# An early-fusion transformer block on one core: probabilities transposed two steps at a time into two banks, and two banks left for all other jobs

## The reference

```
h = concat(tok(x), txt)                      # 32 x 114 x 256
a = layernorm(h)
q, k, v = a@Wq, a@Wk, a@Wv                   # 16 heads of 64
attn = softmax(mask(q k^T / 8)) v            # causal
h = h + (a + attn @ Wo)
r = layernorm(h)
gates = softmax(r @ router_w + router_b)     # 8 experts, the best two are taken
# each expert takes at most 570 tokens, in order of their place
y = sum over chosen experts: gate * (gelu(r @ w1 + b1) @ w2 + b2)
h = h + y
```

## Time and profile before

| | |
|---|---|
| median of 3 runs | 895.91 us |
| profiled execution, its time | 895.53 us |
| its span, first to last instruction | 893.0 us |
| PE busy | 845.5 us (95%) |
| DVE / ACT / POOL busy | 563.9 / 509.0 / 375.0 us |
| PE's share of the chain of waits that ended last | 79% |
| mean granted clock of PE | 0.98 of full speed |
| attention and routing | about 26 to 655 us |
| experts | about 655 to 893 us |

### The profile page before, as it was taken

The page is one execution under the profiler, slowest core; times in us unless marked ns, Lnnn a source line. Parts: engine busy times, 40 slices in busy tenths (PEclk is TensorE's granted clock), DMA queues, the critical chain, the costliest instruction groups (busy, mean ns, idle before and its releaser), DMA issues.

```text
span 893.0 us, 20355 instructions
## 1 busy us (share of the span) xinstructions
PE 845.5 (95%) x7103; PEld 766.9 (86%) x7103; DVE 563.9 (63%) x2466; ACT 509.0 (57%) x1696; POOL 375.0 (42%) x678
## 2 busy tenths in 40 slices
PE   6899999999999999999999999998569999999996
PEld 6788898888889889888888987988559999999995
DVE  3567438567674854856667486477547877668771
ACT  3478656656674765665567367466045655556551
POOL 2144324254553634635454373465523223431334
PEclk9899999999999999999999999999879999999998
DMA  8434220021002102102100100010346545543322
GB/s 227 108 94 129 71 60 17 2 61 44 19 23 72 30 1 67 44 12 53 42 19 16 35 23 2 8 33 3 93 138 183 132 105 138 123 130 100 69 28 28
DMA packets 61959, 57.69 MB, mean 65 GB/s; under 512 B 26831, under 2 KB 56699, under 8 KB 61744
## 3 DMA queue, kind: packets, MB, share of 16 engines
q1 hardware_dynamic: 41218, 45.15, 16.7%
q0 software_dynamic: 18944, 9.76, 6.8%
q10 hardware_dynamic: 1696, 1.49, 0.7%
HBM read 34.25 MB, written 21.89 MB: 63 GB/s over the span
## 4 chain that ended last, share of the span: by engine, by line
PE 79%; DVE 12%; issue 2%; ACT 2%; DMA 2%; POOL 1%; ACTq 1%; POOLq 0%; SPq 0%; DVEq 0%
PE bank L406 14%; PE bank L407 14%; PE bank L408 14%; PE o_bank L1299 5%; PE score_bank L1279 5%; PE pT_bank L1288 4%; PE bank L1178 3%; DVE sm L1009 2%; PE o_bank L407 2%; PE o_bank L408 2%; PE o_bank L406 2%; PE score_bank L406 2%; PE score_bank L407 2%; PE score_bank L408 2%; PE bank L1248 1%
## 5 line engine op out<-in xcount | busy, mean ns | idle before, releaser
L595 POOL TENSOR_SCALAR pr<-pr,rc 114x114 f32<-114x114 f32 x512 | 180.9, 370 | 305.2 <-DVE rc L1049 304.3
L731 ACT ACTIVATE pr<-sm,nb 114x114 f32<-114x114 f32 x512 | 192.3, 383 | 7.4 <-DVE nb L1013 7.3
L1009 DVE CUSTOM_DVE_ANT_0 sm<-score_bank,mask 114x114 f32<-114x114 f32 x512 | 109.9, 273 | 49.5 <-PE score_bank L1279 49.5
L625 POOL DMA_INDIRECT out_dram<-yout,dest x40 | 74.0, 1850 | 159.8 <-ACT yout L777 158.3
L406 PE MATMUL bank<-xT_hi,wqkv_hi 128*128 128x456 f32 (+1 forms) x288 | 110.8, 385 | 3.4 <-ACT xT_hi L645 1.6
L725 ACT ACTIVATE pT<-pT_bank 114x456 f32<-114x456 f32 x128 | 70.6, 551 | 54.3 <-PE pT_bank L1288 54.0
L407 PE MATMUL bank<-xT_lo,wqkv_hi 128*128 128x456 f32 (+1 forms) x288 | 100.2, 348 | 0.0
L408 PE MATMUL bank<-xT_hi,wqkv_lo 128*128 128x456 f32 (+1 forms) x288 | 100.1, 347 | 0.0
L731 ACT ACTIVATION_READ_ACCUMULATOR pr<-sm,nb 114x1 f32 x512 | 99.1, 193 | 0.0
L706 ACT ACTIVATE oT_hi<-o_bank 128x228 fp32r<-128x228 f32 x128 | 45.4, 355 | 85.7 <-PE o_bank L1299 75.9
L1288 PE MATMUL pT_bank<-ident,pr 114*114 114x114 f32 x512 | 74.4, 267 | 0.7 <-ACT pT L725 0.7
(11 more groups left out here) (203 smaller groups left out, 2262.2 us busy)
## 6 DMA issues: line engine op xcount, KB each, us to landing
stage_a<-in_L_ffn_w_dram SPq DMA_DIRECT2D x8, 1024.0 KB
stage_b<-in_L_ffn_w_dram SPq DMA_DIRECT2D x8, 1024.0 KB
slots_dram<-fill SPq DMA_DIRECT2D x8, 605.6 KB
pix<-in_x_dram SPq DMA_DIRECT2D x96, 36.0 KB, 2.3
xs<-slots_dram SPq DMA_DIRECT2D x8, 363.4 KB
hraw<-in_txt_dram SPq DMA_DIRECT2D x8, 308.0 KB
out_dram<-h SPq DMA_DIRECT2D x8, 308.0 KB
xs<-slots_dram SPq DMA_DIRECT2D x8, 242.2 KB
```

The source lines that it names most:

```text
L595: p = pool.tensor_scalar(pr[:, m % 4, i, :], pr[:, m % 4, i, :], rc[:, m % 4, i:i + 1], 1.0, ALU.mult, ALU.mult)
L625: pool.indirect_dma_start(out, bass.IndirectOffsetOnAxis(ap=dest[e % 2][:, t:t + 1], axis=0), yout[:, t, :], None, compute_op=ALU.add).the ...
L731: a = act.activation(pr[:, N % 4, i, :], sm[:, N % 2, i, :], ACT.Exp, bias=nb[:, N % 2, i:i + 1], scale=SCALE, accum_out=rs[:, N % 4, i:i ...
L1009: m = dve.tensor_tensor_reduce(sm[:, N % 2, i, :], score_bank[i % 2][0:T, o:o + T], mask[:, :], 1.0, NEG, ALU.add, ALU.max, mx[:, N % 2, i ...
```

## The change

Six things change.

- The two K and Q tiles become one tile `qk`. In the last group the K and the Q projection of one pair of heads go side by side into one bank as one job QK (456 columns); one drain empties it, by ACT for even and by DVE for odd numbers. 32 jobs become 16.
- `bank` has two banks instead of three, and the probabilities have two, `pT_bank[m % 2]`. Job i now waits for the drain of job i-2.
- PE transposes the probabilities of steps N-3 and N-2 together, in even steps. In odd steps there are none. The transposition of step m waits for the copy of step m-2 instead of m-1.
- In group 6 the logits of group 5 (job L) move from n = 11 to n = 13, between X and the projection; the routing parts that follow move from steps 12, 14, 15 to 14, 15, 15.
- POOL makes the last two images' `rstd` after the fourth of group 6's eight scatters instead of after the eighth.
- The slots are read and cleared with a partition's 5 rows contiguous in DRAM ("(p t)" instead of "(t p)"): runs of 3,264 and 2,176 bytes on load instead of 1,088.

```
@@ -117,8 +117,8 @@
...
         xT_lo = place("xT_lo", [128, KC, GT], F32R)
-        qT = place("qT", [128, 2, GT])
-        kT = place("kT", [128, 2, GT])
+        qk = place("qk", [128, 2, 2, GT])
+        qT, kT = qk[:, 0], qk[:, 1]
         vv = place("vv", [T, GB, HD])
@@ -200,9 +200,9 @@
...
-        bank = [psum(f"bank{i}") for i in range(3)]
+        bank = [psum(f"bank{i}") for i in range(2)]
         score_bank = [psum(f"score_bank{i}") for i in range(2)]
-        pT_bank = psum("pT_bank")
+        pT_bank = [psum(f"pT_bank{i}") for i in range(2)]
         o_bank = [psum(f"o_bank{i}") for i in range(2)]
@@ -246,11 +246,15 @@
...
         ROUTE_NOW, ROUTE_NEXT = {12: (0,), 14: (1,), 15: (2,)}, {0: 3, 1: 4, 3: 5}
-        ROUTE_LAST = {12: (0,), 13: (1, 2), 14: (3, 4)}
+        ROUTE_LAST = [{14: (0,), 15: (1, 2)}, {12: (0,), 13: (1, 2), 14: (3, 4)}]
         AT_C = 2
...
         AT_HALF_O = 14
+
+        def logits_at(g):
+
+            return AT_L if g + 1 != LAST else AT_X
@@ -286,14 +290,11 @@
...
                 return [(name, c)]
-            return [("K", HP * LAST + u), ("Q", HP * LAST + u)] if u in range(PAIRS) else []
-
-        def qk_at(c):
-
-            u = c - HP * LAST
-            if u < 0:
-                return slice(0, GT), c % HP, c % 2, slice(0, GT)
-            return slice(u // HP * 2 * T, (u // HP + 1) * 2 * T), u % HP, u // 2 % 2, slice(u % 2 * 2 * T, (u % 2 + 1) * 2 * T)
+            return [("QK", u)] if u in range(PAIRS) else []
+
+        def last_cols(u):
+
+            return u // 2 % 2, slice(u % 2 * 2 * T, (u % 2 + 1) * 2 * T)
@@ -310,7 +311,9 @@
...
                     jobs.append(("M", g + 2, "d"))
-                jobs += [(name, c, {"K": "a", "Q": "d"}[name]) for name, c in qk_jobs(PAIRS * g + n)]
+                if n == logits_at(g) == AT_X:
+                    jobs.append(("L", g - 1, "d"))
+                jobs += [(name, c, {"K": "a", "Q": "d", "QK": "ad"[c % 2]}[name]) for name, c in qk_jobs(PAIRS * g + n)]
                 jobs += [("V", 2 * GB * f + 2 * b, "a") for f, b in value_jobs(g, n)]
@@ -318,7 +321,7 @@
...
                     jobs += [("Y", KC * (g - 1), "a"), ("Y", KC * (g - 1) + 1, "d")]
-                if n == AT_L and g > 0:
+                if n == logits_at(g) == AT_L and g > 0:
                     jobs.append(("L", g - 1, "d"))
@@ -367,7 +370,7 @@
...
         NF, NX = 2 * MC, len(XJOBS)
-        ebanks = bank + score_bank + [pT_bank] + o_bank
+        ebanks = bank + score_bank + pT_bank + o_bank
@@ -460,8 +463,8 @@
...
                 for e in range(E):
-                    sp.dma_start(slots[e * CAP:(e + 1) * CAP, :].rearrange("(t p) r -> p t r", p=T), fill[:, :, :]).then_inc(slots_cleared, 16)
-                sp.dma_start(out[B * T:B * T + CAP, :].rearrange("(t p) r -> p t r", p=T), fill[:, :, 0:D]).then_inc(slots_cleared, 16)
+                    sp.dma_start(slots[e * CAP:(e + 1) * CAP, :].rearrange("(p t) r -> p t r", p=T), fill[:, :, :]).then_inc(slots_cleared, 16)
+                sp.dma_start(out[B * T:B * T + CAP, :].rearrange("(p t) r -> p t r", p=T), fill[:, :, 0:D]).then_inc(slots_cleared, 16)
@@ -491,7 +494,7 @@
...
             def load_slots(e):
-                rows_of = slots[e * CAP:(e + 1) * CAP, :].rearrange("(t p) r -> p t r", p=T)
+                rows_of = slots[e * CAP:(e + 1) * CAP, :].rearrange("(p t) r -> p t r", p=T)
                 for part, (t0, nt) in enumerate(SLOT_PARTS):
@@ -611,8 +614,9 @@
...
             for i in range(TOPK * GB):
+                if i == TOPK * GB // 2:
+                    rstd(SECOND_HALF, vareps2, rstd2_done, ve2, rstd2, unit_slice(SECOND_HALF))
                 dispatch(LAST - 1, i)
-            rstd(SECOND_HALF, vareps2, rstd2_done, ve2, rstd2, unit_slice(SECOND_HALF))
             for i in range(TOPK * 2):
@@ -649,8 +653,11 @@
...
             def drain_k(c):
-                _, _, i, cols = qk_at(c)
-                drain("K", c, kT[:, i, cols], job_bank("K", c)[:, 0:cols.stop - cols.start])
+                drain("K", c, kT[:, c % 2, :], job_bank("K", c)[:, 0:GT])
+
+            def drain_qk(u):
+                i, cols = last_cols(u)
+                drain("QK", u, qk[:, :, i, cols], job_bank("QK", u)[:, 0:GT].rearrange("p (w t) -> p w t", w=2))
@@ -712,6 +719,8 @@
...
                             drain_k(c)
+                        if name == "QK" and c % 2 == 0:
+                            drain_qk(c)
                     if N > 0:
@@ -722,7 +731,7 @@
...
                     act.wait_ge(pT_done, m + 1)
-                    act.activation(pT[:, m % 2, :, :], pT_bank[0:T, 0:4 * T].rearrange("p (i q) -> p i q", i=4), ACT.Copy).then_inc(pT_copied, 1)
+                    act.activation(pT[:, m % 2, :, :], pT_bank[m % 2][0:T, 0:4 * T].rearrange("p (i q) -> p i q", i=4), ACT.Copy).then_inc(pT_copied, 1)
                 if N < STEPS:
@@ -731,7 +740,7 @@
...
                     a.then_inc(exp_done, 1)
-                if 0 < g < G and n == AT_L + 1:
+                if 0 < g < G and n == logits_at(g) + 1:
                     router_exp(g - 1)
@@ -813,8 +822,11 @@
...
             def drain_q(c):
-                _, _, i, cols = qk_at(c)
-                drain("Q", c, qT[:, i, cols], job_bank("Q", c)[:, 0:cols.stop - cols.start])
+                drain("Q", c, qT[:, c % 2, :], job_bank("Q", c)[:, 0:GT])
+
+            def drain_qk(u):
+                i, cols = last_cols(u)
+                drain("QK", u, qk[:, :, i, cols], job_bank("QK", u)[:, 0:GT].rearrange("p (w t) -> p w t", w=2))
@@ -1019,6 +1031,8 @@
...
                             drain_q(c)
+                        if name == "QK" and c % 2 == 1:
+                            drain_qk(c)
                     if n - 1 - AT_V2 in range(GB):
@@ -1028,7 +1042,7 @@
...
                             drain_y(g - 1)
-                        if n == AT_L + 1:
+                        if n == logits_at(g) + 1:
                             route(g - 1, 0)
@@ -1061,8 +1075,8 @@
...
                         normalise_rows(g - 1, b)
-                    if n != AT_L + 1:
-                        for part in (ROUTE_NOW if g < LAST else ROUTE_LAST).get(n, ()):
+                    if n != logits_at(g) + 1:
+                        for part in (ROUTE_NOW if g + 1 < LAST else ROUTE_LAST[g + 1 - LAST]).get(n, ()):
                             route(g - 1, part)
@@ -1204,14 +1218,26 @@
...
-                if c % HP == 0 and c <= HP * LAST:
+                if c % HP == 0:
                     tokens_split(c // HP)
-                tokens, chunk, _, cols = qk_at(c)
-                dst = claim(name, c)[:, 0:cols.stop - cols.start]
-                col = (0 if name == "Q" else HD) + chunk * 128
+                dst = claim(name, c)[:, 0:GT]
+                col = (0 if name == "Q" else HD) + c % HP * 128
                 for k in range(KC):
                     m = halves(dst, (wqkv_hi[:, k, col:col + 128], wqkv_lo[:, k, col:col + 128]),
-                               (xT_hi[:, k, tokens], xT_lo[:, k, tokens]), k == 0, k == KC - 1, pe)
+                               (xT_hi[:, k, :], xT_lo[:, k, :]), k == 0, k == KC - 1, pe)
+                m.then_inc(filled, 1)
+
+            def project_last(u):
+
+                if u == 0:
+                    tokens_split(LAST)
+                dst = claim("QK", u)
+                tokens = slice(u // HP * 2 * T, (u // HP + 1) * 2 * T)
+                for w in range(2):
+                    col = w * HD + u % HP * 128
+                    for k in range(KC):
+                        m = halves(dst[:, w * 2 * T:(w + 1) * 2 * T], (wqkv_hi[:, k, col:col + 128], wqkv_lo[:, k, col:col + 128]),
+                                   (xT_hi[:, k, tokens], xT_lo[:, k, tokens]), k == 0, k == KC - 1, pe)
                 m.then_inc(filled, 1)
@@ -1266,9 +1292,8 @@
...
-                    for d in (HP * f + c,) if f < LAST else (HP * f + N % PAIRS, HP * f + N % PAIRS + 1):
-                        wait_all(pe, drained("K", d))
-                        wait_all(pe, drained("Q", d))
+                    for job in (("K", HP * f + c), ("Q", HP * f + c)) if f < LAST else (("QK", N % PAIRS), ("QK", N % PAIRS + 1)):
+                        wait_all(pe, drained(*job))
                     if N > 0:
@@ -1282,10 +1307,10 @@
...
                 pe.wait_ge(normed, m + 1)
-                if m > 0:
-                    pe.wait_ge(pT_copied, m)
+                if m > 1:
+                    pe.wait_ge(pT_copied, m - 1)
                 for i in range(4):
-                    p = pe.transpose(pT_bank[0:T, i * T:(i + 1) * T], pr[:, m % 4, i, :], ident[0:T, 0:T])
+                    p = pe.transpose(pT_bank[m % 2][0:T, i * T:(i + 1) * T], pr[:, m % 4, i, :], ident[0:T, 0:T])
                 p.then_inc(pT_done, 1)
@@ -1345,13 +1370,20 @@
...
                             weigh_values(m)
-                if LAG_T <= N < STEPS + LAG_T:
-                    transpose_probs(N - LAG_T)
+                if n % 2 == 0:
```

(12 more changed lines are left out.)

## The result

| | before | after |
|---|---|---|
| median of the runs | 895.94 us (893.94 to 898.15, n = 4) | 955.62 us (955.19 to 956.11, n = 4) |
| ratio, 95% interval | | 1.0666 (1.0644 to 1.0688) |
| span | 893.0 us | 954.3 us |
| PE busy | 845.5 us | 862.0 us |

What follows compares the result with a forecast made beforehand. PE, busy 845.5 of 893.0 us, was taken to bound the kernel. From 895.53 us, 26.5 + 22.5 + 7.5 - 1.2 - 3.2 - 1.5 - 2.0 = +48.6 gave 944 us, range 913 to 963.

Steps and rivals of the forecast that it cites:

- Step 5: Groups 1 to 5: PE, about to fill O, waits for ACT's drain of K; 5.3 us each, 26.5 us (20 to 29).
- step 3: Its wait costs nothing extra in groups 1 to 5, as PE then waits less in step 5; group 6 0.9 us.
- PE's clock: Slow clock after the five new step 5 standstills: 1.5 us each, 7.5 us (0 to 17).
- The other small waits: Bank waits in steps 1, 6, 10, 13, 15, group 6's step 3 and the kernel's start: 22.5 us (8 to 30).
- Pairing: Probabilities' transposes only in even steps: saves 0.02 us in each of some 57 pairs, -1.2 us (bounds 0 and 5).
- Group 6: Logits moved to step 13 fill PE's wait for X, -1.5 us; slow clock stretch behind them goes, -1.7 us.
- Joint drains: QK drains halved in count with the same number of matmuls: costed at nothing.
- The tail: Behind the last step: earlier rstd -1.5 us (0 to -3.3), slots' load -2.0 us (0 to -2.5), load under 5 us.
- two banks are enough: Rival: ACT gives K's bank back before PE comes, only the gains are left: 888 us, faster; chance 0.05.
- Only step 5: Rival: only step 5's wait costs, the other waits are absorbed and the clock holds: 914 us; chance 0.12.
- The clock did not go on falling: Rival judged: small waits bring slow stretches too, some 12 more at 1.7 us: 965 us; chance 0.08.
- the one of step 1: K waits for Q's drain from group 2 on, 5 x 0.45 = 2.3 us; it also delays the pixel loads.

Runs made afterwards that it cites:

- experiment 3: The changed kernel with ACT's pixel rearrangement in step 6 instead of step 4, behind K's drain: 923.65 us, ratio 1.035.
- experiment 9: The kernel of experiment 1 with ACT's pixel rearrangement in step 6 instead of step 4: 887.37 us, ratio 0.9949.
- experiment 4: The changed kernel with 42 extra unused matmuls between V and O in step 5 of groups 1 to 5: 968.83 us, ratio 1.0851.
- experiment 5: The kernel of experiment 4 with 19 extra matmuls per place instead of 42: 948.32 us, ratio 1.0614.
- Experiment 2: The kernel before with two job banks instead of three, the third idle, nothing else changed: 966.93 us, ratio 1.0829.
- experiment 6: The kernel of experiment 1 with group 5's logits back in step 11 of group 6, one run: 887.15 us.
- experiment 8: The kernel of experiment 1 with the slots read and cleared as before, in runs of 1,088 bytes, one run: 889.64 us.
- experiment 1: The changed kernel with three job banks, one probabilities bank and transposes in every step again, the other edits kept: 886.67 us, ratio 0.9934.
- experiment 7: The kernel of experiment 1 with the last rstd behind all eight scatters again, one run: 889.84 us.

## Why the prediction was right, and where its size was off

- *Step 5* was right in place, mechanism and size: forecast 5 x 5.3 = 26.5 us of waiting, measured 25.7 behind what step 3 had already taken of it (5.67, 4.42, 5.08, 5.05 and 5.47, from the distance of the two starts around the wait less the usual 0.23). Experiments 3 and 9 show the cause by taking it away.
- *PE's clock*: forecast 7.5. The O job took 7.29 to 8.50 us in these groups instead of 5.83, which makes 9.2; experiment 4 gives 8.9. Part of the slow stretches fell into the standstill, as I had assumed, 4.2 us of them; but two of the five were 6.8 us long instead of 3.4, and 19.7 us of low clock were left with PE at work. With the waits that makes 34.9, and steps 4/5 show 33.3; the 1.6 between them are the four waits of step 4 that are gone (4 x 0.38).
- *Step 3* was right too. The prediction said that PE, held up there, would wait less in step 5 and that this wait does not delay the loads, so that it costs nothing in groups 1 to 5. PE does wait 0.65 us [the row at 289.85], and steps 2/3 cost 0.86 in each of groups 2 to 6. But the residual sum that releases the loads starts at 289.22, before that wait ends, and K's drain does not move with PE. In group 3 it ends 23.60 us behind the first score of step 2 before (281.22) and 23.69 after (308.64); the mean over groups 2 to 5 is 23.64 before and 23.62 after. From there on PE's start of O is fixed, however long it waited in step 3. Steps 2 to 5 of the five groups together lost 36.8 us, forecast 34.0: 1.7 of the difference are the clock's, 1.1 are the size of the wait, which by K's drain is 5.5 us a group where I had 5.3. The two rows from which the 23 us are counted:

```profile
257.62 1.06 PE L1279 MATMUL score_bank<-kT,qT 64*114 64x114 f32 x16
284.95 1.06 PE L1304 MATMUL score_bank<-qk 64*114 64x114 f32 x16
```

- *The other small waits* were all there and each larger: per group 0.78 against 0.45 in steps 10/11, 0.77 against 0.7 in 6/7, 0.9 against 0.85 in 14/15, and 3.4 against 2 at the start. Without steps 2/3 of groups 2 to 5, which come back, they came to 26.9 (22.5 forecast, bounds 8 and 30). The 2 at the start was an estimate from the like waits, and experiments 3 to 5 show 2.0 to 2.3 there, so most of that excess is this execution's own.
- *Pairing* was forecast at -1.2 us from the removed switches. Where no bank is waited for (steps 8/9) it gives 0.01 us. Experiment 2 shows that elsewhere it makes the waits longer, by 1.2 us a group (the 0.39 of them in steps 2/3 comes back in step 5): the even step's job is filled 0.39 us later, behind the four extra transposes, and so is drained later. It is no gain here; what it would be with enough banks is open.
- *Group 6*: the logits' place is worth 1.0 us (experiment 6), not 1.5. The slow stretch at 530 did vanish in the changed kernel, but such a stretch came back in experiment 8, with the logits in their new place, and stayed away in experiment 6, with the logits in the old one. So the other 1.7 is chance, not an effect of the edit.
- *Joint drains* were put at nothing because DVE and ACT have time to spare. They are worth 2.3 us with three banks (the last group gains them in experiments 1 and 6 to 9 alike, so they are not the logits', the `rstd`'s or the layout's) and some 9.5 with two. What counts is not how busy the drainers are, it is how late the one drain ends that PE waits for: from step 14 of group 6 on PE waited 1.3 us for K's drain with three banks before, and 0 in experiment 1.
- *The tail*: `rstd` is worth 2.1 us, not 1.5. The slots' layout is worth 0.2, not 2.0, and the load took 6.06 us, not under 5: the estimate by the pace of another transfer failed, and the Trainium skill ("DMA: Bandwidth & Descriptors", Specifications), which puts the least size for full rate at 512 bytes, agrees with the measurement.
- *The rivals*: *two banks are enough* is refuted; experiment 3 shows that step 5 alone does not decide it either, since the small waits leave the kernel 3.5% slower without it. The rule of the Trainium skill ("Perfetto Trace Analysis", Matmuls) that groups rotate through different banks is kept by both kernels and does not tell them apart. *Only step 5* is refuted, since of the small waits only step 3's was absorbed. The clock did not go on falling: apart from the five places the slow stretches of the changed kernel are as long as before (at the start two of 3.4 us instead of one of 6.8), without the one at 530.
- *Together*, the 12.7 us by which the traces exceed the forecast are no single step: 4.6 are gains that did not come (pairing, group 6, the tail), 4.8 are small waits, 2.8 are steps 2 to 5 of groups 1 to 5, and 0.5 is the rest.

## What to carry to other kernels

Count banks by the latest drain, not by the busiest engine: for each job set PE's arrival against the end of the drain that its bank needs, and look in the drainer's in-order queue for whatever waits for a DMA in front of it. A wait that is free with one more buffer can be the costliest instruction with one less, and moving it two steps is then worth more than any trimming. A small wait is absorbed by a later, larger one only if the work that ends the larger one was set off before the small one; the wait of step 3 was absorbed because the residual sum that releases the pixel loads did not hang on it, the one of step 1 was not.

## What the runs showed of the hardware that was not expected

- A matmul with both operands in f32 shows as two: 42 instructions gave 84 matmuls, a start every 0.11 us, of 56 columns each (experiment 4). The eight score products of two steps show as 16 in the same way; the f32 transposes of the probabilities show once.
- A slow stretch at a step-5 wait of 4.4 to 5.7 us begins between 2.9 us before PE starts again and 0.7 us after, lasts 3.4 or 6.8 us, and costs the O job 1.5 to 2.7 us. Single ones come without such a wait too, at another place in each run (155.7 in experiment 7, 534.0 in experiment 8, 566.6 in experiment 3), which moves one profile against another by 1 to 3 us.
- The slots' load took 6.27 us in runs of 1,088 bytes and 5.97 to 6.06 in runs two and three times as long.
